# Four of nine FFN down products per chunk as three half products, with one slot more of lag

## The chip, the cores and the metric

The kernel runs on one core of one Trainium2 chip. The time is the device time of one execution in microseconds (us). The core has five engines with a queue of instructions each: TensorE (PE: matmuls; its weight loads stand apart as PEld), VectorE (DVE), ScalarE (ACT), GpSimd (POOL) and SyncE (SP), which here only issues DMAs. An engine takes its instructions strictly in the order in which the program wrote them, and waits on semaphores between them.

## The reference

`x` is 32 x 256 x 128 in float32, that is 8192 tokens of 128 features. What is computed:

```
xn   = layernorm(x)
h,g  = split(xn @ W_hg)                     # 256 + 256
rec  = scan over time: r_t = (1-sigmoid(g_t)) * r_(t-1) + sigmoid(g_t) * (relu(h_t)+0.5)
s    = rec @ W_out
probs = softmax(xn @ Wr)                    # 16 experts, top 2 kept: cw
ffn  = (silu(xn@Sg) * (xn@Su)) @ Sd + sum_e cw_e * (silu(xn@Wg_e) * (xn@Wu_e)) @ Wd_e
out  = x + s * silu(ffn)
```

Two experts of 64 hidden features are handled together as one block of 128, so there are 8 expert blocks and the shared block: nine products `f = 0..8`, each with a gate, a linear and a down product.

## The kernel before

The tokens go in 16 chunks of 512 (`CT`), features on the 128 partitions. The program is written out by hand as one queue per engine. `chunks()` emits chunks 0 and 1, a loop over pairs of chunks, and the last two. Each chunk has 11 slots, `k = 0..10`. In every slot TensorE does `up(k)`: a gate and a linear product, each as three matmuls of float32r halves (`split_product`, lines 604 to 609: hi*hi, lo*hi, hi*lo; x and the weights stand as a rounded high half and a remainder). Slots 0 and 1 are the recurrent part, slots 2 to 10 the nine FFN products, `f = k - 2`. Gates and linears have two PSUM buffers each, so `up(k)` waits for what read the buffers of `up(k-2)`: ScalarE's `silu` (line 319) for the gate, VectorE's `gated` (line 435: `prod = p_lin * silu_g`) for the linear. VectorE's `weighted` (line 445) multiplies `prod` by the expert weight `cw` in SBUF, in place; both of its inputs are in SBUF.

The down product of `f` (line 677) is one float32 matmul of 512 columns (the trace shows it as two records). It accumulates in `p_ffn` and stands `LAG = 3` slots after the product's own slot: at the end of PE slot `f + 5`, so that `f = 6, 7, 8` fall in slots 0, 1, 2 of the next chunk. Its hidden rows come from `weighted`.

Around the chunk boundary, with `ch` the chunk in hand:

- slot 0: TensorE transposes x of the next chunk into `p_front` (L616), which needs `xn`, normalised by VectorE in slots 8 and 9 of the chunk before (L397). ScalarE copies it out (`x_hi`, L297), then does `rec_in(0)` (L302, L304, L307, L309); VectorE does `x_lo` (L404).
- slots 1 and 2: router logits on TensorE (L622), copied by ScalarE (`copy_lgT`, L323), transposed by TensorE (L630). `rec_in(1)` is ahead of that copy in ScalarE's queue.
- after the last down product of the former chunk ScalarE does `ffn_silu` (L340) and VectorE `gate_out` (L508: `sg = p_rec * ffn_gate`). `rec_down(0)` (L687, PE slot 4) overwrites `p_rec` and so waits for `gate_out`. `transpose_out` (L697) and VectorE's `add_out` (L514) follow.
- slot 4 on VectorE: `ln_stats` (L381) of the chunk after the next waits for `x_in` from HBM. The router's steps on the next chunk (L450 to L501) stand between the products. ScalarE's `router_silus` (L328) waits for VectorE's L462, which is behind `ln_stats`, and `silu(5)` is behind `router_silus`.
- slot 10: TensorE transposes the expert weights (L638), ScalarE copies them (L336), and SP writes them to HBM and spreads them over the partitions with four DMAs (L223, 512 KB each). The next `x_in` (L188) is issued behind those on the same SP queue.
- GpSimd only does `rstd_of` (two instructions on 4 columns, L252 and L254) once a chunk.

Of the kernel before, what the change touches and what calls it, by code (L numbers as in the profile page):

```python
# [17 lines left out]
SLOTS = NH + NF  # L18
LAG = 3


class Chunk:
# [17 lines left out]
def recurrent_moe_block(nc, x, W_hg, W_out, Wr, Wg, Wu, Wd, Sg, Su, Sd, out):  # L40
# [13 lines left out]
    with ExitStack() as ctx:  # L54
        def sb(name, shape, dt=F32):
            return ctx.enter_context(nc.sbuf_tensor(name, shape, dt))

        def sem(name):
            return ctx.enter_context(nc.semaphore(name))
# [174 lines left out]
        @block.gpsimd  # L234
        def _(pool):
            nc.gpsimd.memset(minus_half[:, :], -0.5).then_inc(s_const, 1)
            nc.gpsimd.memset(ident[:, :], 0.0).then_inc(s_const0, 1)
            pool.wait_ge(s_const0, 1)
            nc.gpsimd.affine_select(out=ident[:, :], in_=ident[:, :], compare_op=ALU.not_equal, fill=1.0, base=0,
                                    pattern=[[-1, P]], channel_multiplier=1).then_inc(s_const, 1)  # L240
            nc.gpsimd.iota(iota_e[:, :], [[1, E]], base=0, channel_multiplier=0,
                           allow_small_or_imprecise_dtypes=True).then_inc(s_const, 1)
            for col, value in enumerate((-1.0, 1.0, 0.5)):
                nc.gpsimd.memset(consts[:, col:col + 1], value).then_inc(s_const, 1)
            nc.gpsimd.memset(eps[:, :], 1e-5).then_inc(s_const, 1)
# [11 lines left out]
            rstd_of(Chunk(0, 1))  # L257

            def chunk(ch, c):
                if has(c, 2):  # L260
                    rstd_of(ch.at(2))

            chunks(pool, chunk)

        @block.scalar
        def _(act):
# [65 lines left out]
            def copy_cwT(ch, reused):  # L332
# [2 lines left out]
                    act.wait_ge(s_cws, ch.at(-1).n(16, 16))  # L335
                nc.scalar.activation(cwT[:, :], p_out[0:E * TT, 0:P], ACT.Copy).then_inc(s_cwT, 1)  # L336

            def ffn_silu(ch):
                act.wait_ge(s_down, ch.n(NF, NF))
                nc.scalar.activation(ffn_gate[:, :], p_ffn[:, :], ACT.Silu).then_inc(s_gsil, 1)  # L340
# [10 lines left out]
            def chunk(ch, c):  # L351
                late = 1 if c == 0 else 0
                for k in range(SLOTS):
                    if c == 0 and k == 1:
                        router_silus(ch)
                        split_hi(("g", "u"))
                        copy_cwT(ch, False)
                    if k == late and has(c, 1):
                        x_hi(ch.at(1))
                    if k == 2 + late and has(c, 1):  # L360
                        copy_lgT(ch.at(1))
                    if k == 3 and has(c, -1):
                        ffn_silu(ch.at(-1))
                    if k == 5 and has(c, 1):
                        router_silus(ch.at(1))
                    if k < NH:
                        rec_in(ch, k)
                    else:
                        silu(ch, k, c)
                    if k == 10 and has(c, 1):  # L370
                        copy_cwT(ch.at(1), True)

            chunks(act, chunk)
            ffn_silu(Chunk(NCH // 2 - 1, 1))

        @block.vector
        def _(dve):
# [164 lines left out]
            def chunk(ch, c):  # L542
                ahead, ahead2, behind = has(c, 1), has(c, 2), has(c, -1)
                late = 1 if c == 0 else 0
                for k in range(SLOTS):
# [3 lines left out]
                        rec_scan(ch, k - 1)  # L549
                    if c == 0 and k == 1:  # L550
                        split_lo(("u",))
                    if k == 3 and behind:
                        gate_out(ch.at(-1))
                    if k == 5 and behind:
                        add_out(ch.at(-1))
                    if k == 5 and ahead2:
                        ln_stats_landed(ch.at(2))
# [41 lines left out]
        def _(pe):  # L599
# [66 lines left out]
            def down(ch, k, c):  # L666
# [39 lines left out]
            def chunk(ch, c):  # L706
                ahead, behind = has(c, 1), has(c, -1)
                late = 1 if c == 0 else 0
                for k in range(SLOTS):
# [10 lines left out]
                        transpose_logits(ch.at(1))  # L720
                    if k < LAG and behind:
                        down(ch.at(-1), k - LAG + SLOTS, None)
                    if k == 4 and behind:
                        transpose_out(ch.at(-1), True)
                    if k in (4, 5):
                        rec_down(ch, k - 4, c)
# [33 lines left out]
```

## Time and profile before

| | us |
|---|---|
| median of 3 runs | 468.7 (466.78 to 469.61) |
| the profiled execution | 468.29 |
| its span, first to last instruction | 466.5 |
| TensorE busy | 439.5 (94%) |
| VectorE busy | 347.2 (74%) |
| ScalarE busy | 200.0 (43%) |
| GpSimd busy | 25.4 (5%) |

The columns of the timelines shown below are: start in us from the span's start, duration in us, engine, line, operation, output<-inputs, shapes, count, and in brackets the idle time before it and who ended it. Matmul durations include a modelled tail of the pipeline, so the time a matmul takes from its engine is read from start to start.

### The profile page before, as it was taken

The numbers are of one execution on the slowest core, as the hardware profiler recorded it, in microseconds if no ns is written. First come the engines' busy times: TensorE is split into PE (matmuls) and PEld (weight loads), VectorE is DVE, ScalarE is ACT, GpSimd is POOL, SyncE is SP. The second block draws the span as 40 slices with busy tenths as digits, with TensorE's granted clock in tenths as the row PEclk, the third lists the DMA queues.
The fourth block names the chain that finished last, engine by engine and source line by source line (L and its number), as shares of the span: only waits on it lengthen the run. The fifth ranks groups of instructions, "written<-read, shape, count | busy, mean of one in ns | idle before, by whom it ended". The sixth has DMA issues, their size and how long they took to land.

```text
span 466.5 us, 6269 instructions
## 1 busy us (share of the span) xinstructions
PE 439.5 (94%) x1648; PEld 286.4 (61%) x1648; DVE 347.2 (74%) x983; ACT 200.0 (43%) x375; POOL 25.4 (5%) x45
## 2 busy tenths in 40 slices
PE   0787999999899999999999999999999999999995
PEld 0454666656566665666666666666656666666762
DVE  2857678697677968777796877769687776977663
ACT  2722634336163352725335272633527263362621
POOL 1101000010100101010010101001010100100000
PEclk9988999999999999999999999999999999999999
DMA  9091461907528092552809255280925528081640
GB/s 213 22 194 31 102 148 36 196 22 154 98 59 168 25 194 54 125 125 56 171 25 194 53 132 118 58 169 25 193 54 130 120 57 171 26 184 43 140 90 22
DMA packets 50204, 48.98 MB, mean 105 GB/s; under 512 B 6416, under 2 KB 33680, under 8 KB 50192
## 3 DMA queue, kind: packets, MB, share of 16 engines
q1 hardware_dynamic: 44032, 46.67, 46.3%
q10 hardware_dynamic: 6160, 2.17, 2.3%
q8 instruction: 5, 0.08, 0.1%
q14 instruction: 7, 0.06, 0.0%
HBM read 44.11 MB, written 4.72 MB: 105 GB/s over the span
## 4 chain that ended last, share of the span: by engine, by line
PE 56%; DMA 19%; SPq 4%; DVE 2%; issue 2%; ACT 2%; ACTq 0%
PE p_ffn L677 17%; DMA x_in<-in_L_attn_x 16%; PE p_gate L607 6%; PE p_lin L607 6%; PE p_lin L609 5%; PE p_gate L608 5%; PE p_gate L609 5%; PE p_lin L608 5%; SPq L223 4%; DMA cw_scratch<-cwT 3%; PE p_rec L687 3%; ACT silu_g L319 1%; DVE stats L381 1%; PE p_out L697 1%; DVE prod L445 1%
## 5 line engine op out<-in xcount | busy, mean ns | idle before, releaser
L677 PE MATMUL p_ffn<-prod,w_down 128*128 128x512 f32 x288 | 148.7, 599 | 0.0
L319 ACT ACTIVATE silu_g<-p_gate 128x512 f32<-128x512 f32 x144 | 83.8, 592 | 120.2 <-PE p_gate L609 108.3
L607 PE MATMUL p_gate<-xT_hi,w_hi 128*128 128x512 f32 x176 | 124.3, 707 | 8.3 <-ACT silu_g L319 5.6
L435 DVE TENSOR_TENSOR prod<-p_lin,silu_g 128x512 f32<-128x512 f32 x144 | 97.8, 679 | 12.9 <-PE p_lin L609 9.9
L445 DVE TENSOR_TENSOR prod<-prod,cw 128x512 f32<-128x512 f32 x128 | 86.6, 676 | 4.3 <-DMA cw<-cw_scratch 1.8
L607 PE MATMUL p_lin<-xT_hi,w_hi 128*128 128x512 f32 x176 | 71.7, 407 | 0.0
L609 PE MATMUL p_gate<-xT_hi,w_lo 128*128 128x512 f32 x176 | 70.0, 398 | 0.0
L609 PE MATMUL p_lin<-xT_hi,w_lo 128*128 128x512 f32 x176 | 69.9, 397 | 0.0
L608 PE MATMUL p_gate<-xT_lo,w_hi 128*128 128x512 f32 x176 | 69.8, 397 | 0.0
L608 PE MATMUL p_lin<-xT_lo,w_hi 128*128 128x512 f32 x176 | 69.7, 396 | 0.0
L607 PEld LDWEIGHTS p_gate<-xT_hi,w_hi 128*128 128x128 f32 x176 | 33.6, 191 | 51.9 <-issue 28.6
L677 PEld LDWEIGHTS p_ffn<-prod,w_down 128*128 128x128 f32 x288 | 52.2, 189 | 20.7 <-issue 9.1
L608 PEld LDWEIGHTS p_gate<-xT_lo,w_hi 128*128 128x128 f32 x176 | 33.7, 191 | 31.6 <-issue 30.9
L381 DVE BATCH_NORM_STATS2 stats<-x_in 128x6 f32<-128x128 f32 x64 | 14.0, 280 | 45.4 <-DMA x_in<-in_L_attn_x 45.4
L420 DVE SCALAR_TENSOR_TENSOR rec_v<-rec_v,rec_z 128x512 f32<-128x512 f32 x32 | 22.1, 692 | 33.5 <-ACT rec_z L309 33.5
L328 ACT ACTIVATE silu_n<-shifted,consts 128x64 f32<-128x64 f32 x16 | 5.6, 347 | 84.6 <-DVE shifted L462 84.6
L426 DVE TENSOR_TENSOR_SCAN rec_h<-rec_a,rec_v 128x256 f32<-128x256 f32 x64 | 40.8, 678 | 1.1
L607 PEld LDWEIGHTS p_lin<-xT_hi,w_hi 128*128 128x128 f32 x176 | 33.4, 190 | 11.4 <-DVE prod L435 4.2
L609 PEld LDWEIGHTS p_lin<-xT_hi,w_lo 128*128 128x128 f32 x176 | 33.5, 190 | 8.4
L609 PEld LDWEIGHTS p_gate<-xT_hi,w_lo 128*128 128x128 f32 x176 | 33.3, 189 | 7.7
L608 PEld LDWEIGHTS p_lin<-xT_lo,w_hi 128*128 128x128 f32 x176 | 33.5, 190 | 7.3
L687 PE MATMUL p_rec<-rec_h,w_down 128*128 128x512 f32 x64 | 32.7, 592 | 0.0
(60 smaller groups left out, 360.9 us busy)
## 6 DMA issues: line engine op xcount, KB each, us to landing
cw<-cw_scratch SPq DMA_DIRECT2D x64, 512.0 KB, 8.5
x_in<-in_L_attn_x SPq DMA_DIRECT2D x16, 256.0 KB, 10.6
x_out<-in_L_attn_x SPq DMA_DIRECT2D x16, 256.0 KB, 10.6
out_x<-x_out SPq DMA_DIRECT2D x16, 256.0 KB, 2.3
prod<-in_L_ffn_Wg ACTq DMA_DIRECT2D x1, 512.0 KB, 5.9
prod<-in_L_ffn_Wu ACTq DMA_DIRECT2D x1, 512.0 KB, 7.8
w_down<-in_L_ffn_Wd ACTq DMA_DIRECT2D x1, 512.0 KB, 4.5
cw_scratch<-cwT SPq DMA_DIRECT2D x16, 32.0 KB, 1.8
```

Source lines behind the costliest of these rows:

```text
L223: sp.dma_start(cw[e * F:(e + 1) * F, ch.par, b0:b1, :], spread_rows)\
L319: nc.scalar.activation(silu_g[:, par], p_gate[par][:, :], ACT.Silu).then_inc(s_silu, 1)
L381: last = nc.vector.bn_stats(stats[:, t], x_in[:, ch.par, t])
L420: nc.vector.scalar_tensor_tensor(out=rec_v[:, j], in0=rec_v[:, j], scalar=0.5, in1=rec_z[:, j], op0=ALU.add, op1=ALU.mult).then_inc(s_v, 1)
L426: last = nc.vector.tensor_tensor_scan(rec_h[:, j, w], rec_a[:, j, w], rec_v[:, j, w], 0.0, ALU.mult, ALU.add)
L435: nc.vector.tensor_tensor(prod[:, f], p_lin[par][:, :], silu_g[:, par], ALU.mult).then_inc(s_p, 1)
L445: nc.vector.tensor_tensor(prod[:, f], prod[:, f], cw[:, ch.par, f - 1], ALU.mult).then_inc(s_q, 1)
L607: nc.tensor.matmul(acc, w_hi[:, w], hi, start=start, stop=False)
L608: nc.tensor.matmul(acc, w_hi[:, w], lo, start=False, stop=False)
L609: return nc.tensor.matmul(acc, w_lo[:, w], hi, start=False, stop=stop)
L677: nc.tensor.matmul(p_ffn[:, :], w_down[:, at0:at0 + P], prod[:, f], start=f == 0, stop=f == NF - 1)\
L687: last = nc.tensor.matmul(p_rec[:, :], w_down[:, at0:at0 + P], rec_h[:, j], start=j == 0, stop=j == NH - 1)
```

## The change

- `SPLIT = (2, 4, 6, 8)`: the down products of these four `f` are done as three float32r matmuls into the same `p_ffn`: hi weight * hi product, lo weight * hi product, hi weight * lo product.
- The high half of the product (`prod_hi`) is a copy by ScalarE, from SBUF to SBUF; the low half (`prod_lo = prod - prod_hi`) a subtraction by GpSimd with both inputs in SBUF. Both have two buffers. The halves of the weights are made once, at the start.
- The copy for `f` stands in ScalarE's queue at slot `f + 3`, behind that slot's `silu`; for `f = 8` that is slot 0 of the next chunk, between `rec_in(0)` and `rec_in(1)`.
- `LAG = 4`: every down product stands one slot later on TensorE. `ffn_silu` and `gate_out` move from slot 3 to 4, `transpose_out` from 4 to 5, `add_out` from 5 to 6. `rec_down` stays in slots 4 and 5.
- GpSimd's `rstd_of` now stands behind the first of the four subtractions of its chunk.

```diff
-LAG = 3
+LAG = 4
+SPLIT = (2, 4, 6, 8)
...
+            def product_lo(ch, n, c):
+                f = SPLIT[n]
+                pool.wait_ge(s_phi, ch.n(NS, n + 1))
+                if n >= 2:
+                    pool.wait_ge(s_down, ch.n(NF, SPLIT[n - 2] + 1))
+                elif has(c, -1):
+                    pool.wait_ge(s_down, ch.at(-1).n(NF, SPLIT[n + NS - 2] + 1))
+                nc.gpsimd.tensor_tensor(prod_lo[:, n % 2], prod[:, f], prod_hi[:, n % 2].bitcast(F32), ALU.subtract)\
+                  .then_inc(s_plo, 1)
+
             def chunk(ch, c):
-                if has(c, 2):
-                    rstd_of(ch.at(2))
+                for n in range(NS):
+                    if n == 1 and has(c, 2):
+                        rstd_of(ch.at(2))
+                    product_lo(ch, n, c)
...
+            def product_hi(ch, n, known):
+                f = SPLIT[n]
+                act.wait_ge(s_q, ch.n(NB, f))
...
+                nc.scalar.activation(prod_hi[:, n % 2], prod[:, f], ACT.Copy).then_inc(s_phi, 1)
...
-                    if k == 3 and has(c, -1):
+                    if k == 4 and has(c, -1):
                         ffn_silu(ch.at(-1))
...
+                    if k == 0 and has(c, -1):
+                        product_hi(ch.at(-1), NS - 1, True)
+                    for n, f in enumerate(SPLIT):
+                        if k == f + NH + 1:
+                            product_hi(ch, n, has(c, -1))
...
-                    if k == 3 and behind:
+                    if k == 4 and behind:
                         gate_out(ch.at(-1))
-                    if k == 5 and behind:
+                    if k == 6 and behind:
                         add_out(ch.at(-1))
...
+                elif f in SPLIT:
+                    n = SPLIT.index(f)
...
+                    pe.wait_ge(s_plo, ch.n(NS, n + 1))
+                    w = slice(n * P, (n + 1) * P)
+                    nc.tensor.matmul(p_ffn[:, :], down_hi[:, w], prod_hi[:, n % 2], start=False, stop=False)
+                    nc.tensor.matmul(p_ffn[:, :], down_lo[:, w], prod_hi[:, n % 2], start=False, stop=False)
+                    nc.tensor.matmul(p_ffn[:, :], down_hi[:, w], prod_lo[:, n % 2], start=False, stop=f == NF - 1)\
+                      .then_inc(s_down, 1)
+                    return
...
-                    if k == 4 and behind:
+                    if k == 5 and behind:
                         transpose_out(ch.at(-1), True)
```

**TensorE, slots 3 and 4 of a chunk in the loop.** Six matmuls with `p_gate` and `p_lin` are one `up`; in brackets stands what an instruction waits for. Before, from the end of `up(2)`'s down product on:

```order
L607 MATMUL p_gate<-xT_hi,w_hi 128x512 [waits tanh_done]
L608 MATMUL p_gate<-xT_lo,w_hi 128x512
L609 MATMUL p_gate<-xT_hi,w_lo 128x512
L607 MATMUL p_lin<-xT_hi,w_hi 128x512 [waits relu_done]
...
L607 MATMUL p_gate<-xT_hi,w_hi 128x512 [waits silu_done]
...
L607 MATMUL p_lin<-xT_hi,w_hi 128x512 [waits gated_done]
...
L695 REGISTER_ALU [waits sg_done]
L697 MATMUL p_out<-ident,sg 128x128 [waits cwT_copied]
L697 MATMUL p_out<-ident,sg 128x128 x3
L687 MATMUL p_rec<-rec_h,w_down 128x512 [waits scan_done,sg_done]
```

and now, for the same two slots:

```order
L658 MATMUL p_gate<-xT_hi,w_hi 128x512 [waits tanh_done]
...
L658 MATMUL p_lin<-xT_hi,w_hi 128x512 [waits relu_done]
...
L731 MATMUL p_ffn<-prod_hi,down_hi 128x512 [waits product_lo_ready]
L732 MATMUL p_ffn<-prod_hi,down_lo 128x512
L733 MATMUL p_ffn<-prod_lo,down_hi 128x512
L658 MATMUL p_gate<-xT_hi,w_hi 128x512 [waits silu_done]
...
L658 MATMUL p_lin<-xT_hi,w_hi 128x512 [waits gated_done]
...
L749 MATMUL p_rec<-rec_h,w_down 128x512 [waits scan_done,sg_done]
```

The last down product of the former chunk (`f = 8`) now stands behind `up(3)`. Before, two `up`s stood between it and the first instruction that waits for `sg`; now it is one.

**VectorE, slots 3 and 4 of the same chunk.** Before:

```order
L435 TENSOR_TENSOR prod<-p_lin,silu_g 128x512 [waits linear_in_psum]
L506 REGISTER_ALU
L508 TENSOR_TENSOR sg<-p_rec,ffn_gate 128x512 [waits rec_out_done,ffn_gate_done]
L434 REGISTER_ALU [waits silu_done]
L435 TENSOR_TENSOR prod<-p_lin,silu_g 128x512 [waits linear_in_psum]
L450 TENSOR_REDUCE lg<-p_front 128x64 [waits router_logits]
L453 ISA
L445 TENSOR_TENSOR prod<-prod,cw 128x512 [waits gated_done,cw_first_half1,router_step]
L457 MAX top<-lg 128x8 x4
```

and now:

```order
L486 TENSOR_TENSOR prod<-p_lin,silu_g 128x512 [waits linear_in_psum]
L501 TENSOR_REDUCE lg<-p_front 128x64 [waits router_logits]
L504 ISA
L496 TENSOR_TENSOR prod<-prod,cw 128x512 [waits gated_done,cw_first_half1,router_step]
L508 MAX top<-lg 128x8 x4
L557 REGISTER_ALU
L559 TENSOR_TENSOR sg<-p_rec,ffn_gate 128x512 [waits rec_out_done,ffn_gate_done]
```

`sg` was made ahead of `gated(3)`; now it comes behind `gated(3)`, the router's sum, `weighted(3)` and the router's maximum.

**ScalarE, slots 0 and 1.** Now (before, the rows with `prod_hi` and the REGISTER_ALU ahead of it were not there):

```order
L336 ACTIVATE rec_z<-rec_z,consts 128x512
L373 REGISTER_ALU
L378 ACTIVATE prod_hi<-prod 128x512 [waits down_done,weighted_done]
L328 REGISTER_ALU
L329 ACTIVATE rec_z<-p_gate 128x512 [waits gate_in_psum]
L331 ACTIVATE rec_v<-p_lin 128x512 [waits linear_in_psum]
L333 REGISTER_ALU
L334 ACTIVATE rec_a<-rec_z,consts 128x512 [waits tanh_done]
L336 ACTIVATE rec_z<-rec_z,consts 128x512
L350 ACTIVATE lgT<-p_front 32x512 [waits router_logits_T]
```

The copy for `f = 8` stands ahead of `rec_in(1)` and of the copy of the logits, which TensorE's L630 (now L681) waits for.

## Rows read from the trace of the kernel before

**Rows 1.** The page, busy time and share of the span.

```profile
PE 439.5 (94%) x1648; PEld 286.4 (61%) x1648; DVE 347.2 (74%) x983; ACT 200.0 (43%) x375; POOL 25.4 (5%) x45
```

**Rows 2.** Timeline of TensorE, a down product and the gate product behind it.

```profile
210.47 1.02 PE L677 MATMUL p_ffn<-prod,w_down 128*128 128x512 f32 x2
...
211.55 0.39 PE L608 MATMUL p_gate<-xT_lo,w_hi 128*128 128x512 f32 x1
211.78 0.40 PE L609 MATMUL p_gate<-xT_hi,w_lo 128*128 128x512 f32 x1
```

**Rows 3.** The page, chain of work that ended last, shares of the span.

```profile
PE 56%; DMA 19%; SPq 4%; DVE 2%; issue 2%; ACT 2%; ACTq 0%
```

**Rows 4.** The waits, in total, times and longest.

```profile
DVE stats L381 <- DMA x_in<-in_L_attn_x: 45.4, 15, 4.5
```

**Rows 5.** Timeline of TensorE, the transposition of the expert weights, once a chunk.

```profile
214.96 0.27 PE L638 MATMUL p_out<-ident,cw_tok 128*128 128x128 f32 x1
242.14 0.27 PE L638 MATMUL p_out<-ident,cw_tok 128*128 128x128 f32 x1
...
405.31 0.27 PE L638 MATMUL p_out<-ident,cw_tok 128*128 128x128 f32 x1
432.05 0.27 PE L638 MATMUL p_out<-ident,cw_tok 128*128 128x128 f32 x1
```

**Rows 6.** Timeline of TensorE in the chunk from 214.96 on.

```profile
222.83 0.43 PE L630 MATMUL p_front<-ident,lgT 32*128 32x32 f32 x4
...
226.93 0.60 PE L697 MATMUL p_out<-ident,sg 128*128 128x128 f32 x4
...
232.72 1.02 PE L677 MATMUL p_ffn<-prod,w_down 128*128 128x512 f32 x2
233.72 0.50 PE L607 MATMUL p_gate<-xT_hi,w_hi 128*128 128x512 f32 x1
```

**Rows 7.** Timeline of ScalarE in the same chunk.

```profile
221.32 0.71 ACT L309 ACTIVATE rec_z<-rec_z,consts 128x512 f32<-128x512 f32 x1
221.94 0.57 ACT L323 ACTIVATE lgT<-p_front 32x512 f32<-32x512 f32 x1
...
233.09 1.06 ACT L319 ACTIVATE silu_g<-p_gate 128x512 f32<-128x512 f32 x2
```

**Rows 8.** Timeline of VectorE in the same chunk.

```profile
224.98 0.69 DVE L508 TENSOR_TENSOR sg<-p_rec,ffn_gate 128x512 f32<-128x512 f32 x1 [0.33 <-ACT ffn_gate L340]
225.76 0.69 DVE L435 TENSOR_TENSOR prod<-p_lin,silu_g 128x512 f32<-128x512 f32 x1
...
227.61 0.67 DVE L435 TENSOR_TENSOR prod<-p_lin,silu_g 128x512 f32<-128x512 f32 x1
230.97 0.87 DVE L381 BATCH_NORM_STATS2 stats<-x_in 128x6 f32<-128x128 f32 x4 [2.68 <-DMA x_in<-in_L_attn_x]
...
233.07 0.67 DVE L514 TENSOR_TENSOR x_out<-p_out,x_out 128x512 f32<-128x512 f32 x1
233.85 0.69 DVE L435 TENSOR_TENSOR prod<-p_lin,silu_g 128x512 f32<-128x512 f32 x1
...
235.02 0.66 DVE L445 TENSOR_TENSOR prod<-prod,cw 128x512 f32<-128x512 f32 x1
...
235.73 0.68 DVE L435 TENSOR_TENSOR prod<-p_lin,silu_g 128x512 f32<-128x512 f32 x1
...
241.51 0.59 DVE L397 TENSOR_SCALAR xn<-x_in,meanvar,rstd 128x128 f32<-128x128 f32 x2
```

**Rows 9.** Timeline of GpSimd, start of the program and the same chunk.

```profile
1.22 0.29 POOL L239 TENSOR_SCALAR_AFFINE_SELECT ident<-ident 128x128 f32<-128x128 f32 x1 [0.24 <-POOL ident L237]
...
5.48 0.20 POOL L252 TENSOR_TENSOR var_eps<-meanvar,eps 128x4 f32<-128x4 f32 x1 [3.64 <-DVE meanvar L389]
...
235.18 0.55 POOL L252 TENSOR_TENSOR var_eps<-meanvar,eps 128x4 f32<-128x4 f32 x1 [25.54 <-DVE meanvar L389]
```

**Rows 10.** Timeline of TensorE, the last four down products of the program.

```profile
457.33 3.59 PE L677 MATMUL p_ffn<-prod,w_down 128*128 128x512 f32 x8
```

More of the change, by code:

```diff
@@ L99, in recurrent_moe_block @@
         rec_h = sb("rec_h", [P, NH, CT])
+        NS = len(SPLIT)
+        down_hi = sb("down_hi", [P, NS * P], F32R)
+        down_lo = sb("down_lo", [P, NS * P], F32R)
+        prod_hi = sb("prod_hi", [P, 2, CT], F32R)
+        prod_lo = sb("prod_lo", [P, 2, CT], F32R)
         silu_g = sb("silu_g", [P, 2, CT])
@@ L154, in recurrent_moe_block @@
         s_down = sem("down_done")
+        s_dwhi, s_dwlo = sem("down_weights_hi"), sem("down_weights_lo")
+        s_phi, s_plo = sem("product_hi_ready"), sem("product_lo_ready")
         s_rec, s_gsil, s_sg, s_ot, s_add = (sem("rec_out_done"), sem("ffn_gate_done"), sem("sg_done"),
@@ L257, in _ @@
             rstd_of(Chunk(0, 1))
+            for n, f in enumerate(SPLIT):
+                w = slice(down_at["d"] + (f - 1) * P, down_at["d"] + f * P)
+                pool.wait_ge(s_dwhi, n + 1)
+                nc.gpsimd.tensor_tensor(down_lo[:, n * P:(n + 1) * P], w_down[:, w],
+                                        down_hi[:, n * P:(n + 1) * P].bitcast(F32), ALU.subtract).then_inc(s_dwlo, 1)
+            def product_lo(ch, n, c):
[7 more added lines that the diff above has]
+                  .then_inc(s_plo, 1)
             def chunk(ch, c):
-                if has(c, 2):
-                    rstd_of(ch.at(2))
+                for n in range(NS):
+                    if n == 1 and has(c, 2):
+                        rstd_of(ch.at(2))
+                    product_lo(ch, n, c)
             chunks(pool, chunk)
@@ L336, in copy_cwT, with down_weights_hi @@
                 nc.scalar.activation(cwT[:, :], p_out[0:E * TT, 0:P], ACT.Copy).then_inc(s_cwT, 1)
+            def down_weights_hi():
+                act.wait_ge(s_w["d"], 16)
+                for n, f in enumerate(SPLIT):
+                    w = slice(down_at["d"] + (f - 1) * P, down_at["d"] + f * P)
+                    nc.scalar.activation(down_hi[:, n * P:(n + 1) * P], w_down[:, w], ACT.Copy).then_inc(s_dwhi, 1)
+            def product_hi(ch, n, known):
+                f = SPLIT[n]
+                act.wait_ge(s_q, ch.n(NB, f))
+                if n >= 2:
+                    act.wait_ge(s_down, ch.n(NF, SPLIT[n - 2] + 1))
+                elif known:
+                    act.wait_ge(s_down, ch.at(-1).n(NF, SPLIT[n + NS - 2] + 1))
+                nc.scalar.activation(prod_hi[:, n % 2], prod[:, f], ACT.Copy).then_inc(s_phi, 1)
             def ffn_silu(ch):
@@ L357, in chunk @@
                         copy_cwT(ch, False)
+                    if c == 0 and k == 2:
+                        down_weights_hi()
                     if k == late and has(c, 1):
@@ L371, in chunk @@
                         copy_cwT(ch.at(1), True)
+                    if k == 0 and has(c, -1):
+                        product_hi(ch.at(-1), NS - 1, True)
+                    for n, f in enumerate(SPLIT):
+                        if k == f + NH + 1:
+                            product_hi(ch, n, has(c, -1))
             chunks(act, chunk)
-            ffn_silu(Chunk(NCH // 2 - 1, 1))
+            last = Chunk(NCH // 2 - 1, 1)
+            product_hi(last, NS - 1, True)
+            ffn_silu(last)
         @block.vector
@@ L673, in down @@
                     pe.wait_ge(s_p, ch.n(NF, 1))
+                elif f in SPLIT:
+                    n = SPLIT.index(f)
+                    if c == 0:
+                        pe.wait_ge(s_dwlo, n + 1)
+                    pe.wait_ge(s_plo, ch.n(NS, n + 1))
[5 more added lines that the diff above has]
+                    return
                 else:
```

## The prediction

> **What bounds the kernel now.** I read the page's busy shares first: TensorE 94%, nobody else over 74% [rows 1]. So TensorE looks like the bound, and a change that takes work from it looks good. The chain of waits says less: 56% TensorE, 19% DMA [rows 3]. The list of waits names it: VectorE waits for `x_in` 15 times, 45.4 us in all [rows 4]. The timeline shows what this does. A chunk, measured between two transpositions of the expert weights, takes 242.14 - 214.96 = 27.18 us; the one chunk that loads no `x_in` takes 432.05 - 405.31 = 26.74 [rows 5]. Expert weights, their spread and `x_in` form a line: `x_in` is there 230.97 - 214.96 = 16.01 us after the transposition [rows 5, 8]; then come `ln_stats`, `weighted(4)`, the router's shift, ScalarE's router silus and `silu(5)`, of which TensorE's gate of slot 7 waits until 233.72, while its down product at 232.72 was over 0.86 later, at 233.58 [rows 6]. So a chunk is a stretch A of 18.76 us (to the gate of slot 7), with 18.62 of TensorE's own work and a floor at 18.76 set by the DMAs, and a stretch B of 8.42 us. TensorE's own work in B is four `up`s of 6 x 0.233 = 1.40 and three down products of 0.86, 8.18; the rest, 0.24, is waiting behind the late `silu` and `gated`.
>
> **What it saves.** Start to start, half matmuls are 0.23 apart (211.78 - 211.55). The gate behind the down product began at 211.55 - 0.23 = 211.32, so the float32 product takes 211.32 - 210.47 = 0.85 to 0.86 [rows 2]. Three halves take 0.69 or 0.70. That saves 0.16 each, 64 x 0.16 = 10.2 us in all, if TensorE never waits. Per chunk: three of the four (`f = 4, 6, 8`) fall in A, 0.48, which takes TensorE's work there to 18.14, below the floor; one (`f = 2`) in B.
>
> **ScalarE's copies.** A 512 column instruction from SBUF follows its neighbour by 221.94 - 221.32 = 0.62 [rows 7]; I take 0.61. Three of the four per chunk stand where ScalarE idles. That of `f = 8` does not: it pushes `rec_in(1)` and the copy of the logits. The copy ended at 221.94 + 0.57 = 222.51, just ahead of TensorE's L630 at 222.83 [rows 6, 7]. Now it ends 0.61 later, less the 0.16 by which all of slot 0 is early: 222.96. TensorE has saved two halves' worth by then and wants it at 222.51; it starts at 223.0. **Wait: 0.5.** It could be as little as 0.3 if the copy overlaps its neighbours.
>
> **`sg`.** Slot 3's `up` ended at 226.93 - 1.40 = 225.53; now at 225.53 - 0.32 + 0.5 = 225.7. `gated(3)` started 0.23 after that (225.76), and VectorE was through with slot 3 at 227.61, 1.85 later [rows 8]. Only then comes `gate_out`, 0.69: 225.7 + 0.23 + 1.85 + 0.69 = 228.5. TensorE has `f = 8` (0.69) and `up(4)` (1.40) meanwhile and wants `sg` for `rec_down(0)` at 227.8. **Wait: 0.7**, where before `sg` was ready at 225.67, over 1 us early. It depends on no unknown price. A becomes 18.62 - 0.48 + 0.5 + 0.7 = 19.35, over the floor of 18.76 by 0.6. `x_in` itself stays where it was.
>
> **B without further trouble.** The 0.24 of waiting goes, since TensorE is late itself; one half product: 8.18 - 0.16 = 8.02. A chunk: 19.35 + 8.02 = **27.4**, against 27.18: the whole saving is gone, with 0.2 more.
>
> **GpSimd beside VectorE.** This is the large unknown. The trace has no GpSimd instruction of 512 columns. Its select on 128 columns takes 0.29, some 1.5 ns a column beyond 0.1; its two-input add on 4 columns 0.20 [rows 9]. That makes 0.20 + 512 x 1.5 ns = 1.0 us for a subtraction; bounds are 0.6 (near VectorE's 0.69 for this shape) and 1.7 (each input read in turn). TensorE has over 2 us of slack for each. But the same add takes 0.55 at 235.18: VectorE's `weighted`, two inputs in SBUF, ran from 235.02 to 235.68, and the add ended at 235.73 [rows 8, 9]. GpSimd sat out VectorE's whole instruction; the two exclude each other. The trace cannot show the reverse, as a read of 4 columns holds nothing up. Bounds of what a subtraction costs VectorE: nothing, or its whole duration. I take the exclusion to hold both ways, since it lasted to the end of the holder's instruction.
>
> The subtraction becomes ready about 0.7 after its `weighted`, while VectorE is in the next `gated` (one input in SBUF), and the next `weighted` or mask stands behind it: some 0.85 of 1.0 us each. Three fall in the stretch from `x_in` to the second half of `xn`, the third only partly: C = 2.0 us.
>
> Does VectorE have room for that? From 230.97 to the end of `xn` at 242.10 it hardly pauses [rows 8]. Before, `add_out` (233.07) filled the time until `silu(5)` was over at 233.09 + 0.57 = 233.66, and `gated(5)` started at 233.85 [rows 7, 8]. In the new order `gated(5)` waits for the same `silu(5)`, and `add_out` is paid behind it: some 0.5 later, so `xn` is ready 16.01 + 11.13 + 0.5 + C = 27.6 + C after the transposition. TensorE needs it for the transposition of x, 0.8 after the end of the chunk's period P. If it waits s there, P = 27.4 + s and s = 27.6 + C - P - 0.8, so P = 27.1 + C/2 once C is over 0.6. With C = 2.0: **P = 28.1**.
>
> The Trainium skill, page SBUF — State Buffer, section Who interferes with whom, says that VectorE with two SBUF inputs contends with a GpSimd instruction that reads SBUF, and that whoever issues second fully blocks. This trace agrees in one direction (0.20 against 0.55 us) and shows nothing of the other; by the row alone, with VectorE never blocked, the chunk would stay at 27.4, by the rule it is the 28.1.
>
> The same skill, page GPSIMD Engine Reference, section Performance versus the Vector engine, gives 4497 ns for a two-input add of 2048 columns; a quarter is an estimate of 1.1 us, and no run here shows it. By it the sum would be about 1 us longer.
>
> **The rest.** Thirteen chunks have the steady form (C = 0: 13 x 0.2 = 2.9). Chunk 14 has no `x_in` and loses 1.2 to the two waits against 0.64 saved: +0.6. The last has no router: -0.5; in its tail, four down products took 8 records at 0.43 = 3.43 [rows 10]; now the last `weighted`, 1.7 after slot 10, is followed by copy 0.6, subtraction 1.0 and three halves 0.7, 4.1: +0.7. Weight halves at the start: four small copies and subtractions while TensorE waits anyway, 0. Two late `x_in`s of the thirteen are partly covered now: -0.8. Sum without contention: 2.9 + 0.6 - 0.5 + 0.7 - 0.8 = +2.9. With C = 2.0: 13 x 0.7 = 9.1 more, +12. The profiled execution took 468.29, 0.4 below the median: 480.3 by it, **481** by the median.
>
> **The rivals.** *(1) VectorE isn't blocked*: GpSimd alone gives way. For it: only that direction is in the trace. Then +2.9, **472**. *(2) It pays*: the two waits vanish, because VectorE reaches `gate_out` in time and the logits' copy slips in. Then A sits on its floor of 18.76 and B costs 8.02: 26.78, 13 x -0.4 = -5.2, the ends about -1: **462**. It is decided by `gate_out` ending before 227.8; against it stand three queued VectorE instructions. If even the floor gave way the full saving would lead to 458. *(3) Subtraction at its upper bound of 1.7*: C = 3.5, P = 28.9, **491**.
>
> **Chances.** Forecast (C from 1 to 3, 474 to 488) 0.52; rival 1 0.30; rival 2 0.12; rival 3 0.06. A measurement of this kernel tells about 1%, 4.7 us. The range of 466 to 490 leaves out rival 2 and half of the upper tail. Faster by over 1% (below 464): 0.12. Within 1%: rival 1 but for a rest, 0.28. Slower: 0.60.
>
> **What would show it.** Right: TensorE waits at the transposed logits (L681) some 0.5 and at `rec_down(0)` (L749) some 0.7 a chunk, the latter for `sg`; `weighted` (L496) with durations well over 0.69, or gaps before it; chunk period 28.1. VectorE's wait for `x_in` shrinks. Wrong: `weighted` still at 0.68 throughout (rival 1), no wait at L749 (rival 2), subtractions of more than 1.5 us (rival 3). The prediction also fails if blocking is traded against VectorE's idle time in slots 0 to 4 more than I assume.

## The result: 7% slower, and the profile after

The changed kernel takes 501.49 us (median of 4 runs, 500.56 to 504.06), the kernel before 469.15 (4 runs, 466.78 to 471.53): a ratio of 1.0701, 95% interval 1.0664 to 1.0738. The direction was forecast, the size was not: 32 us were lost where 12 were expected, and the range ended at 490. The profiled execution took 501.97 us with a span of 500.2, against 468.29 and 466.5.

I read the page first: busy times, then the shares of the chain of waits.

```profile
PE 434.4 (87%) x1712; PEld 296.2 (59%) x1712; DVE 410.4 (82%) x983; ACT 231.8 (46%) x443; POOL 111.5 (22%) x113
...
DMA 30%; issue 17%; DVE 17%; PE 9%; ACT 6%; SPq 6%; ACTq 1%; DVEq 0%; POOLq 0%
...
L281 POOL TENSOR_TENSOR prod_lo<-prod,prod_hi 128x512 fp32r<-128x512 f32 x64 | 82.6, 1290 | 352.4 <-ACT prod_hi L378 326.2
...
L496 DVE TENSOR_TENSOR prod<-prod,cw 128x512 f32<-128x512 f32 x128 | 106.5, 832 | 3.9 <-DMA cw<-cw_scratch 1.3
```

VectorE has the same 983 instructions as in [rows 1] and is busy for 410.4 us instead of 347.2. That is 63.2 us more for 64 subtractions on another engine, 1.0 us each. A subtraction takes 1.29 us. TensorE, 56% of the chain in [rows 3], now has 9%: it no longer sets the time, although its queue is busy for 87% of the span.

The waits (in total, times, longest):

```profile
ACT prod_hi L378 <- DVE prod L496: 70.5, 29, 3.7
...
PE p_front L667 <- DVE xn L448: 31.4, 15, 8.1
...
DVE stats L432 <- DMA x_in<-in_L_attn_x: 25.3, 15, 4.0
...
PE p_rec L749 <- DVE sg L559: 9.6, 15, 0.8
...
PE p_front L681 <- ACT lgT L350: 5.3, 14, 0.4
```

The two waits of TensorE that the forecast named are there (0.4 at L681, 0.6 at L749 a chunk), and VectorE's for `x_in` has shrunk from the 45.4 of [rows 4]. On top, TensorE waits for `xn`, and ScalarE's copy waits for `weighted`. The period, by the transposition of the expert weights (timeline of TensorE; compare [rows 5]):

```profile
198.03 0.27 PE L689 MATMUL p_out<-ident,cw_tok 128*128 128x128 f32 x1
...
227.66 0.27 PE L689 MATMUL p_out<-ident,cw_tok 128*128 128x128 f32 x1
...
257.18 0.27 PE L689 MATMUL p_out<-ident,cw_tok 128*128 128x128 f32 x1
```

A chunk takes 29.5 us, not 27.2. This chunk on VectorE (the lines that were stretched, with the `x_in` at either end):

```profile
215.24 0.87 DVE L432 BATCH_NORM_STATS2 stats<-x_in 128x6 f32<-128x128 f32 x4 [1.07 <-DMA x_in<-in_L_attn_x]
...
218.67 1.32 DVE L537 TENSOR_TENSOR mask<-iota_e,top_at 128x64 f32<-128x64 f32 x1
...
224.17 1.84 DVE L496 TENSOR_TENSOR prod<-prod,cw 128x512 f32<-128x512 f32 x1
...
227.37 0.68 DVE L496 TENSOR_TENSOR prod<-prod,cw 128x512 f32<-128x512 f32 x1
228.57 1.69 DVE L448 TENSOR_SCALAR xn<-x_in,meanvar,rstd 128x128 f32<-128x128 f32 x2
...
235.06 2.34 DVE L477 TENSOR_TENSOR_SCAN rec_h<-rec_a,rec_v 128x256 f32<-128x256 f32 x2
238.02 1.27 DVE L477 TENSOR_TENSOR_SCAN rec_h<-rec_a,rec_v 128x256 f32<-128x256 f32 x2
...
244.77 0.87 DVE L432 BATCH_NORM_STATS2 stats<-x_in 128x6 f32<-128x128 f32 x4 [1.12 <-DMA x_in<-in_L_attn_x]
```

and GpSimd in the same stretch:

```profile
218.65 1.27 POOL L281 TENSOR_TENSOR prod_lo<-prod,prod_hi 128x512 fp32r<-128x512 f32 x1 [12.01 <-ACT prod_hi L378]
...
224.16 1.30 POOL L281 TENSOR_TENSOR prod_lo<-prod,prod_hi 128x512 fp32r<-128x512 f32 x1 [2.02 <-PE p_ffn L733]
228.89 1.30 POOL L281 TENSOR_TENSOR prod_lo<-prod,prod_hi 128x512 fp32r<-128x512 f32 x1 [3.43 <-ACT prod_hi L378]
234.98 1.29 POOL L281 TENSOR_TENSOR prod_lo<-prod,prod_hi 128x512 fp32r<-128x512 f32 x1 [4.79 <-ACT prod_hi L378]
```

Each subtraction has one VectorE record beside it that is too long by most of the subtraction's duration: the mask by 1.1 (0.22 otherwise), `weighted` by 1.16 (0.68 at 227.37), `xn` by 1.1 (0.59 in [rows 8]), the scans by 1.07 (1.27 at 238.02). The line behind a stretched record never starts before the subtraction has ended: right at its end behind the mask (219.92) and `xn` (230.19), 0.5 us later behind `weighted`, 1.1 behind the scans. GpSimd blocks VectorE as VectorE blocked GpSimd in [rows 9].

The Trainium skill, page SBUF — State Buffer, section Who interferes with whom, says that the two share a port pair as an exclusive lock, held for the whole instruction by whoever issues first. This trace now agrees in both directions, with 0.68 against 1.84 us for the same shape on VectorE.

**The loop that holds the chunk** goes through the one place where ScalarE's copies hurt (timeline of ScalarE):

```profile
228.09 0.63 ACT L378 ACTIVATE prod_hi<-prod 128x512 fp32r<-128x512 f32 x1 [2.64 <-DVE prod L496]
228.62 0.58 ACT L346 ACTIVATE silu_g<-p_gate 128x512 f32<-128x512 f32 x1
229.10 0.26 ACT L363 ACTIVATE cwT<-p_out 64x128 f32<-64x128 f32 x1
```

`x_in` lands at 215.24. VectorE, blocked twice on the way, reaches the end of the `weighted` of 227.37 at 228.05. ScalarE has stood 2.64 us at `prod_hi` for `f = 6` for it. Behind that in its queue are `silu(10)` and `copy_cwT`, though TensorE's transposition was done shortly after 227.66. `copy_cwT` releases the expert weights' spread and, on the same SP queue, the next `x_in`, which lands 15.67 us after 229.10. So 215.24 to 229.10 is 13.86, and 13.86 + 15.67 = 29.53, the period. TensorE is not in this loop. Measured from the transposition, `x_in` lands 244.77 - 227.66 = 17.11 us later, in the kernel before 16.01.

### The profile page after: what moved, and what is told of

It is laid out like the page before. It is cut to its first block, busy times and chain, and to the rows that moved or that the text cites. A ratio compares the mean times of both kernels' runs of the same rounds, so it can differ in the third digit from the quotient of the medians.

```text
span 500.2 us, 6755 instructions
## 1 busy us (share of the span) xinstructions
PE 434.4 (87%) x1712; PEld 296.2 (59%) x1712; DVE 410.4 (82%) x983; ACT 231.8 (46%) x443; POOL 111.5 (22%) x113
## 4 chain that ended last, share of the span: by engine, by line
DMA 30%; issue 17%; DVE 17%; PE 9%; ACT 6%; SPq 6%; ACTq 1%; DVEq 0%; POOLq 0%
DMA x_in<-in_L_attn_x 24%; SPq L232 5%; DMA cw_scratch<-cwT 4%; DVE prod L496 4%; ACT silu_g L346 4%; DVE prod L486 3%; DVE xn L448 2%; DVE x_out L565 2%; DVE stats L432 2%; DMA cw<-cw_scratch 1%; PE p_ffn L739 1%; PE p_rec L749 1%; PE p_gate L660 1%; PE p_gate L658 1%; PE p_gate L659 1%
## 5 line engine op out<-in xcount | busy, mean ns | idle before, releaser
L281 POOL TENSOR_TENSOR prod_lo<-prod,prod_hi 128x512 fp32r<-128x512 f32 x64 | 82.6, 1290 | 352.4 <-ACT prod_hi L378 326.2
L658 PE MATMUL p_gate<-xT_hi,w_hi 128*128 128x512 f32 x176 | 115.0, 653 | 6.0 <-ACT silu_g L346 3.2
L496 DVE TENSOR_TENSOR prod<-prod,cw 128x512 f32<-128x512 f32 x128 | 106.5, 832 | 3.9 <-DMA cw<-cw_scratch 1.3
L739 PE MATMUL p_ffn<-prod,w_down 128*128 128x512 f32 x160 | 83.6, 604 | 0.0
L378 ACT ACTIVATE prod_hi<-prod 128x512 fp32r<-128x512 f32 x64 | 40.0, 625 | 72.1 <-DVE prod L496 70.5
L477 DVE TENSOR_TENSOR_SCAN rec_h<-rec_a,rec_v 128x256 f32<-128x256 f32 x64 | 56.9, 929 | 1.1
L749 PE MATMUL p_rec<-rec_h,w_down 128*128 128x512 f32 x64 | 34.3, 617 | 9.6 <-DVE sg L559 9.6
L667 PE MATMUL p_front<-ident,xn 128*128 128x128 f32 x64 | 10.9, 294 | 31.8 <-DVE xn L448 31.4
```

The lines of the kernel that those rows point to most:

```text
L281: nc.gpsimd.tensor_tensor(prod_lo[:, n % 2], prod[:, f], prod_hi[:, n % 2].bitcast(F32), ALU.subtract)\
L378: nc.scalar.activation(prod_hi[:, n % 2], prod[:, f], ACT.Copy).then_inc(s_phi, 1)
L477: last = nc.vector.tensor_tensor_scan(rec_h[:, j, w], rec_a[:, j, w], rec_v[:, j, w], 0.0, ALU.mult, ALU.add)
L496: nc.vector.tensor_tensor(prod[:, f], prod[:, f], cw[:, ch.par, f - 1], ALU.mult).then_inc(s_q, 1)
L658: nc.tensor.matmul(acc, w_hi[:, w], hi, start=start, stop=False)
L739: nc.tensor.matmul(p_ffn[:, :], w_down[:, at0:at0 + P], prod[:, f], start=f == 0, stop=f == NF - 1)\
```

## The experiments

Two theories were open at first: the *loop* just read, and *TensorE's own* waits with contention only on top. Each run is set against the kernel before, run on the same chip.

**lo_4cols: contention taken away.** GpSimd subtracts 4 columns.

```
-                nc.gpsimd.tensor_tensor(prod_lo[:, n % 2], prod[:, f], prod_hi[:, n % 2].bitcast(F32), ALU.subtract)\
+                nc.gpsimd.tensor_tensor(prod_lo[:, n % 2, 0:4], prod[:, f, 0:4], prod_hi[:, n % 2, 0:4].bitcast(F32), ALU.subtract)\
```

> The changed kernel, but GpSimd subtracts only the first 4 of the 512 columns of each product (the low half of the other columns stays zero, so the output lacks those corrections); every wait, copy and matmul is kept. It takes the 1.1 us blocks of VectorE away (the subtraction is about 0.2 us long) and nothing else. Theory (GpSimd holding VectorE up carries nearly all of the loss; the two new waits of TensorE cost 0.2 us a chunk): 470 to 475 us, as the forecast's sum without contention, 472. Rival (the lag, ScalarE's copies and the longer queue carry a good part): 480 us or more, with TensorE still waiting for xn at the transposition of x.

475.40 us, ratio 1.0146 (1.0107 to 1.0185); period 27.5. VectorE busy is 348.1, back at that of before. The edit also makes the subtraction itself shorter, but TensorE waits for `prod_lo` only once in the changed kernel, 0.5 us at the end. So 26 of the 32 us are contention. What is left fits the forecast's chunk without contention, 27.4, and TensorE's waits are those it named (waits):

```profile
PE p_rec L754 <- DVE sg L564: 9.7, 15, 0.8
...
PE p_front L686 <- ACT lgT L355: 5.3, 14, 0.4
```

It also gives the length of the loop (timelines of VectorE and ScalarE, in this order):

```profile
233.34 0.88 DVE L437 BATCH_NORM_STATS2 stats<-x_in 128x6 f32<-128x128 f32 x4 [2.09 <-DMA x_in<-in_L_attn_x]
...
244.07 0.63 ACT L383 ACTIVATE prod_hi<-prod 128x512 fp32r<-128x512 f32 x1 [1.55 <-DVE prod L501]
```

From `x_in` to this copy 244.07 - 233.34 = 10.73, in the changed kernel 228.09 - 215.24 = 12.85. The two blocks inside cost 2.12 of the 2.26 by which their records are longer, and 29.5 - 2.1 = 27.4: by this sum the loop without them is about as long as TensorE's chunk, so that every further block in it counts in full.

**lag4_only: the later slot alone**, the kernel before with `LAG = 4` and the four slots moved.

```
-LAG = 3
+LAG = 4
```

> The kernel before with LAG = 4 and the four stages moved with it; no halves, nothing new on ScalarE or GpSimd. Theory: rec_down(0) waits for sg, since VectorE reaches gate_out 2.8 us after up(3) and TensorE gets there in 2.3; 0.4 to 0.6 us a chunk, of which 0.14 was waiting before: 471 to 476 us. Rival (the expert weights and x_in set the pace and hide it): 468 to 470.

475.81 us, 1.0151 (1.0113 to 1.0189); period 27.5. The wait for `sg` is there without any copy or subtraction:

```profile
PE p_rec L687 <- DVE sg L508: 6.5, 14, 0.6
```

The later slot loses 7 us by itself. lo_4cols, which has it too, saves 0.64 a chunk on TensorE, but waits 0.4 for the logits and 0.65 instead of 0.46 for `sg`, and so takes the same time.

**split_lag3: the split without the later slot.** `ffn_silu`, `gate_out`, `transpose_out` and `add_out` are back in their slots of before.

```
-LAG = 4
+LAG = 3
```

> The changed kernel with LAG = 3 and ffn_silu, gate_out, transpose_out and add_out in their slots of before; halves, copies and subtractions kept. Theory (the loop through VectorE, ScalarE and the DMAs sets the period, so TensorE's waits for sg, 0.7 us a chunk, cost nothing now): 498 to 503 us, as the changed kernel, with no wait at rec_down(0). Rival (each of TensorE's waits adds to the sum): 489 to 492.

492.86 us, 1.0517 (1.0470 to 1.0564): 9 less than the change. The theory missed (498 to 503), and the time is within 1 us of what the rival named (489 to 492: each of TensorE's waits adds), so it does not decide between them. The chain of waits does (page); it is still that of the loop:

```profile
DMA 28%; DVE 21%; issue 17%; PE 12%; ACT 6%; SPq 6%; ACTq 0%; DVEq 0%; POOLq 0%; POOL 0%
```

I had missed where `add_out` goes (timeline of VectorE):

```profile
211.23 0.87 DVE L432 BATCH_NORM_STATS2 stats<-x_in 128x6 f32<-128x128 f32 x4 [1.81 <-DMA x_in<-in_L_attn_x]
...
213.34 0.67 DVE L565 TENSOR_TENSOR x_out<-p_out,x_out 128x512 f32<-128x512 f32 x1
...
240.24 0.87 DVE L432 BATCH_NORM_STATS2 stats<-x_in 128x6 f32<-128x128 f32 x4 [1.96 <-DMA x_in<-in_L_attn_x]
```

`add_out` is back where VectorE waits anyway (in the change it stands at 221.06, inside the loop). `copy_cwT` is at 224.49, 13.26 behind `x_in` instead of 13.86. The DMAs then take 240.24 - 224.49 = 15.75, so this chunk is 29.0 long instead of 29.5: 13 x 0.5 = 6.5 of the 9.

**cwT_first: the loop's ScalarE part cut.** `prod_hi` of `f = 6` goes behind `silu(10)` and `copy_cwT`.

```
-                        if k == f + NH + 1:
+                        if k == f + NH + (2 if f == 6 else 1):
```

> The changed kernel, but ScalarE's copy of the product f = 6 stands one slot later, behind the copy of the transposed expert weights (cwT) instead of ahead of it. Theory (a loop without TensorE sets the period: x_in lands, VectorE works to weighted(8), ScalarE's copy waits for it with silu(10) and the copy of cwT queued behind it, so SP issues the next x_in late): the cwT copy starts 0.4 us after TensorE's transposition instead of 1.4, x_in comes 1 us earlier, and the chunk falls from 29.5 to 28.5 to 28.9 us: 488 to 494 us. Rival (the copy of cwT is late but not on the path, as VectorE's own blocks set the pace through xn): 500 to 502, unchanged.

489.36 us, 1.0429 (1.0381 to 1.0477); period about 28.5. One copy moved, 12 us back. Timelines of TensorE, ScalarE, VectorE and GpSimd, in this order:

```profile
223.60 0.27 PE L689 MATMUL p_out<-ident,cw_tok 128*128 128x128 f32 x1
...
223.99 0.27 ACT L363 ACTIVATE cwT<-p_out 64x128 f32<-64x128 f32 x1 [0.36 <-PE p_out L689]
...
224.51 0.59 DVE L448 TENSOR_SCALAR xn<-x_in,meanvar,rstd 128x128 f32<-128x128 f32 x2
...
226.34 1.07 DVE L496 TENSOR_TENSOR prod<-prod,cw 128x512 f32<-128x512 f32 x1
...
224.95 1.90 POOL L281 TENSOR_TENSOR prod_lo<-prod,prod_hi 128x512 fp32r<-128x512 f32 x1 [3.56 <-ACT prod_hi L378]
```

`copy_cwT` now starts 0.39 after the transposition (in the change 1.44). And the later subtraction meets `xn` second: `xn` keeps its 0.59, it is the subtraction that takes 1.90, and it holds only the `weighted` of 226.34, by 0.4. So the edit shortens the loop's ScalarE part by 1.05 and also takes a block away from `xn`, and the 12 us are not the first alone. That the loop holds the changed kernel rests on its waits, one at each link, and on x_early_after below, where the DMA link alone is cut. What is left here, 20 us, is not split up; TensorE waits for `xn` (17.2 us in 14 times, 8.1 of them once), the logits and `sg`.

**dve_lo: the subtractions on VectorE itself**, one slot behind the copy.

```
-                nc.gpsimd.tensor_tensor(prod_lo[:, n % 2], ...)
+                nc.vector.tensor_tensor(prod_lo[:, n % 2], ...)
```

> The changed kernel, but VectorE does the subtraction itself, behind weighted of slot f + 4 (f = 8: slot 1 of the next chunk); GpSimd is as in the kernel before. VectorE pays 4 x 0.61 = 2.4 us a chunk instead of four blocks of 1.1. Two of the four stand ahead of the second half of xn. Theory (VectorE's time between x_in and xn, and the cwT copy behind the copy of product 6, set the loop): chunk about 27.9 to 28.3, 478 to 485 us, well below the 501 of the changed kernel, with no long weighted. Rival (VectorE's extra work is as bad as GpSimd's blocks): 495 or more.

486.94 us, 1.0375 (1.0352 to 1.0398), a little over what I expected. The instruction takes 681 ns there (group of instructions):

```profile
L562 DVE TENSOR_TENSOR prod_lo<-prod,prod_hi 128x512 fp32r<-128x512 f32 x64 | 43.6, 681 | 0.1
```

VectorE is busy for 383.7 us, 27 less than with the work "taken off" it. GpSimd's help costs VectorE more than doing the work itself, and the kernel 15 us more.

**pool_reads and pool_reads_late: contention alone.** The kernel before, with four GpSimd subtractions of 512 columns a chunk on idle tiles. In the first they are released by `weighted`; in the second three of them by the `gated` behind it, which is about when the change's subtractions start.

```
+                    nc.gpsimd.tensor_tensor(spare[:, :], w_down[:, 0:CT], w_down[:, CT:2 * CT], ALU.subtract)
```

```
-                    pool.wait_ge(s_q, ch.n(NB, 2 * n + 2))
+                    if n < 3:
+                        pool.wait_ge(s_p, ch.n(NF, 2 * n + 4))
+                    else:
+                        pool.wait_ge(s_q, ch.n(NB, NB))
```

> The kernel before, plus four GpSimd subtractions of 512 columns per chunk on spare data (weights in SBUF, result unused), each released by weighted(2), (4), (6), (8). No copy on ScalarE, no change of lag, TensorE's work as before. It measures the disputed cost by itself. Theory (GpSimd's reads hold up VectorE's instructions whatever data they read): weighted, the mask, xn and the scan get durations 0.6 to 1.1 us above their own, and the chunk grows from 27.2 to 27.6 to 28.3 us: 474 to 484 us. Rival (the loss of the changed kernel comes from ScalarE's queue alone): 468 to 471 us.

470.82 us, 1.0020 (0.9996 to 1.0043): my expectation missed, nothing is lost. Timeline of VectorE, then of GpSimd:

```profile
264.38 1.15 DVE L456 TENSOR_TENSOR prod<-prod,cw 128x512 f32<-128x512 f32 x1
...
268.10 1.26 DVE L408 TENSOR_SCALAR xn<-x_in,meanvar,rstd 128x128 f32<-128x128 f32 x2
...
263.71 1.28 POOL L272 TENSOR_TENSOR spare<-w_down 128x512 f32<-128x512 f32 x1 [0.76 <-DVE prod L456]
267.74 1.28 POOL L272 TENSOR_TENSOR spare<-w_down 128x512 f32<-128x512 f32 x1 [2.75 <-DVE prod L456]
```

The subtraction at 263.71 starts right behind a `weighted`, and VectorE is in `gated` (one input from PSUM), untouched. Only the rest of it meets the next `weighted`: 1.15 instead of 0.65. `xn` pays 0.67. That is 1.17 in all, and the kernel takes it up: TensorE waits for `xn` only at the start of the program (waits).

```profile
PE p_front L627 <- DVE xn L408: 8.2, 1, 8.2
```

By the forecast's numbers the room before TensorE waits is 27.18 + 0.8 - (16.01 + 11.13) = 0.84. So I asked whether the start decides:

> The kernel before plus the same four GpSimd subtractions on spare data, but those of products 2, 4 and 6 are released 0.6 us later: by gated of the next slot instead of by weighted itself, which is about where the changed kernel starts them behind ScalarE's copy. Released by weighted they cost nothing (470.8 us). Theory (a subtraction of 1.29 us holds VectorE for what is left of it when VectorE's next instruction with two SBUF inputs, or xn, comes; begun behind weighted half of it passes beside gated, begun behind gated nearly all is waited for): instructions of VectorE stretched by 1.1 to 1.2 us three times between x_in and xn, chunk 27.9 to 28.4: 479 to 487 us. Rival (the placing makes no difference, only ScalarE's queue does): 469 to 473.

480.83 us, 1.0241 (1.0205 to 1.0277); period 28.1. Timeline of VectorE, then of GpSimd:

```profile
266.83 1.53 DVE L459 TENSOR_TENSOR prod<-prod,cw 128x512 f32<-128x512 f32 x1
...
271.55 1.31 DVE L509 TENSOR_TENSOR mask<-mask,expv 128x64 f32<-128x64 f32 x1
...
266.53 1.29 POOL L275 TENSOR_TENSOR spare<-w_down 128x512 f32<-128x512 f32 x1 [15.12 <-DVE prod L449]
```

The same four instructions, three of them started later against VectorE's sequence, cost 10 us: VectorE is busy for 390.7 us, against 362.0 in pool_reads. So the blocks alone, with no copy and no later slot, make the kernel slower.

**x_early_before and x_early_after: the DMA link cut.** SP issues each `x_in` a chunk earlier, behind the store and ahead of the spread of the expert weights, in the kernel before and in the changed one; the loop over chunk pairs ends one pair earlier.

```
-                if has(c, 2):
+                if c == 0:
                     load_x(ch.at(2))
...
                     store(ch.at(-1))
+                if has(c, 3):
+                    load_x(ch.at(3))
```

> The kernel before with x_in loaded one chunk earlier: SP issues it ahead of the spread of the expert weights instead of behind it (the loop is one pair of chunks shorter and that pair written out, for the index). Theory (in the kernel before each chunk pays 0.4 us for x_in being late behind the spread): every chunk takes the 26.7 us of the one that loads no x_in, VectorE's wait for x_in is gone: 459 to 464 us. Rival (something else, the spread itself or VectorE's own work, stands right behind): 466 to 469.

460.36 us, 0.9797 (0.9781 to 0.9813); period 26.75, that of the one chunk without `x_in` in [rows 5]. TensorE has 90% of the chain.

> The changed kernel with x_in loaded one chunk earlier in the same way; GpSimd's subtractions and all else kept. It cuts the loop x_in, VectorE, ScalarE, spread, x_in at one place. Theory (the blocks of VectorE only cost because they stand in that loop; VectorE's idle wait for x_in then takes them in): the chunk falls from 29.5 to 27.2 to 27.7 us, TensorE's own work plus the waits for the logits and sg: 470 to 478 us. Rival (the blocks hit TensorE directly, by xn and gated): 488 or more.

483.40 us, 1.0291 (1.0274 to 1.0309); period about 28.4. The time lies between theory and rival: 18 us are back, with VectorE blocked as before (busy for 409.0 us), but a second loop takes over. Timeline of TensorE, then of VectorE:

```profile
220.95 0.65 PE L671 MATMUL p_front<-ident,xn 128*128 128x128 f32 x4 [0.79 <-DVE xn L452]
249.26 0.65 PE L671 MATMUL p_front<-ident,xn 128*128 128x128 f32 x4 [0.77 <-DVE xn L452]
...
231.07 0.69 DVE L490 TENSOR_TENSOR prod<-p_lin,silu_g 128x512 f32<-128x512 f32 x1 [0.65 <-PE p_lin L664]
...
247.41 1.71 DVE L452 TENSOR_SCALAR xn<-x_in,meanvar,rstd 128x128 f32<-128x128 f32 x2
```

From the transposition of x TensorE takes 10.1 us to the linear product of the VectorE line at 231.07; from there VectorE, blocked three times, takes 18.05 to the end of `xn` at 249.12. With the 0.14 to TensorE that is 28.3. This is not the forecast's path either: that one also ended at `xn`, but it ran through the DMAs and `x_in` and took two chunks (P = 27.1 + C/2).

**x_early_4cols and all_off: is the saving real?** The first is lo_4cols with the early `x_in`. The second also puts the copy for `f = 8` two slots later and `rec_down` one slot later, which takes away TensorE's two waits.

```
-                    if k == 0 and has(c, -1):
+                    if k == 2 and has(c, -1):
                         product_hi(ch.at(-1), NS - 1, True)
...
-                    if k in (4, 5):
-                        rec_down(ch, k - 4, c)
+                    if k in (5, 6):
+                        rec_down(ch, k - 5, c)
```

> The changed kernel with x_in loaded one chunk earlier and GpSimd's subtraction on 4 of the 512 columns (the low half of the other columns stays zero): neither the loop through the DMAs nor the blocks, but both of TensorE's new waits. Theory (what is left are the two waits, 0.4 for the copied logits and 0.75 for sg, against 0.64 saved): chunk 27.2 to 27.4, 468 to 472 us, 8 to 11 above the kernel before with early x_in (460). Rival (the waits are partly the effect of blocks and late x_in): 460 or less.

471.42 us, 1.0032 (1.0015 to 1.0049); period 27.4, against 27.5 in lo_4cols: in both TensorE with its two waits holds the chunk. Of the 4 us between the two, 2 fall in a single chunk near the start (29.20 and 27.33).

> As x_early_4cols, and the two waits taken away too: ScalarE's copy of product 8 stands in slot 2 behind the copy of the logits, and rec_down in slots 5 and 6 instead of 4 and 5. Theory (the saving of 0.16 us per product is real and is seen once nothing else is in the way): chunk 26.75 - 0.64 = 26.1 us, 449 to 453 us. Rival (three half products between other matmuls don't save TensorE 0.16 us): 458 or more.

451.96 us, 0.9609 (0.9581 to 0.9637), 8.4 less than x_early_before:

```profile
233.44 0.27 PE L698 MATMUL p_out<-ident,cw_tok 128*128 128x128 f32 x1
259.54 0.27 PE L698 MATMUL p_out<-ident,cw_tok 128*128 128x128 f32 x1
```

26.1 against 26.75 a chunk: the 4 x 0.16 = 0.64 of the half products, whole, once nothing else is in TensorE's way.

**all_off_real: the same with all 512 columns subtracted.**

> As all_off, but GpSimd subtracts all 512 columns: the whole change, with early x_in, the copy of product 8 behind the logits, and rec_down one slot later. The blocks of VectorE are back, and nothing else. Theory (a second loop holds it: from the transposition of x TensorE needs 9.6 us to lin(3), VectorE from there 18 us to xn, of which 3.3 are blocks): chunk 27.6 to 28.0, 472 to 479 us. Rival (with x_in early VectorE's slack takes the blocks in): under 462.

475.01 us, 1.0112 (1.0081 to 1.0143); period about 27.9. Of TensorE's waits in the loop only that for `xn` is left:

```profile
PE p_front L671 <- DVE xn L452: 27.8, 15, 8.1
```

All the moves that help cannot pay for the subtractions on GpSimd: 23 us between 4 columns and 512. The version that beats both kernels is x_early_before, the kernel before with its `x_in` issued early.

## Why the prediction was right and wrong

**Right.**

- The two waits of TensorE: 0.37 and 0.55 in the chunk shown, against 0.5 and 0.7 forecast. The chunk without contention is 27.5 (lo_4cols), summed as 27.4, and lo_4cols is at 475 where the sum gave 472. lag4_only shows that the later slot brings the `sg` wait.
- The saving of 0.16 a product is real (all_off).
- The exclusion holds both ways; rival 1 (VectorE isn't blocked, 472) falls with the 1.84 us of `weighted`. Rival 2 (the two waits vanish, 462) falls with TensorE's waits. Rival 3 wanted a subtraction over 1.5 us: at 1.29 it isn't that, though its 491 was nearest.

**The step that failed: "`x_in` itself stays where it was".** It rested on "Three of the four per chunk stand where ScalarE idles". That of `f = 6` does stand in idle time, but it *waits* there for `weighted`, with `silu(10)` and `copy_cwT` queued behind it. `copy_cwT` comes 1.44 after the transposition starts instead of 0.39, and the time of `x_in` hangs on VectorE: it lands 17.11 after the transposition, not 16.01. I took P = 27.1 + C/2, a loop in which TensorE passes on half of what VectorE loses. In the one that holds, each block between `x_in` and `prod_hi(6)` counts whole. With my own price of 0.85 for each of the two blocks there, it gives 27.4 + 1.7 = 29.1 where I had 28.1: 13 x 1.0 = 13 us. x_early_after cuts this link, with all blocks kept, and gets 18 us back; cwT_first takes the copy out of the way and gets 12.

**The mis-sized term: the price of a block.** I took 0.85 of a subtraction of 1.0 us; measured are 1.29 and 1.1. The two blocks cost 2.1, not 1.7: 13 x 0.4 = 5 us. C as I defined it, all three up to `xn`, is 1.10 + 1.16 + 1.10 = 3.4, not 2.0; with that, my own formula would give 27.1 + 1.7 = 28.8, 0.7 short of the 29.5 measured: the right price alone would not have mended it. VectorE's path was otherwise as I had it: from `x_in` to the end of `xn` it takes 230.26 - 215.24 = 15.02, and 11.13 + 0.5 + 3.4 is 15.0. The Trainium skill's page GPSIMD Engine Reference, section Performance versus the Vector engine, from which 1.1 us was estimated, is nearer than my 1.0 and still under the 1.29.

**The ends.** Chunk 14, without `x_in`, I had at +0.6; it takes 464.19 - 434.91 = 29.28 against 26.74 [rows 5], +2.5; in it TensorE waits 1.69 for `xn`, which I had not counted there. Behind the last transposition of the expert weights the span has 500.2 - 464.19 = 36.0, before 466.5 - 432.05 = 34.5: +1.5 where I had +0.2 for router and tail. In the tail TensorE waits 0.47 for the last subtraction. (The tail's sum of 4.1 should have been 4.0.) Together the ends make 3 us. With 13 and 5 it is 21 of the 21.7 between the 480.3 forecast for a profiled execution and 501.97.

**A worry that came true the other way round.** That "blocking is traded against VectorE's idle time" holds for pool_reads, where VectorE is only 14.8 us busier and nothing is lost, and not for the change: its subtractions come after ScalarE's copy, just when VectorE turns to its next instruction of the sensitive kind.

**Open.** dve_lo's 28.4 isn't split up; TensorE waits there for `prod_lo` as well (8.7 us in 14 times). A subtraction split into shorter ones was not tried.

## What to carry to other kernels

Work that GpSimd takes over from SBUF isn't off VectorE: price it at up to its full duration there (here 1.1 of 1.29 us), and read from the timeline which instruction it will meet and who starts first. When an instruction that waits is put into an in-order queue, list what is behind it, and follow that through the DMAs to the next round: a loop that bypasses the busiest engine can be the next bound while that engine still shows 87%. Where two loops are about equally long, shortening one gives little: the early `x_in` brings 9 us to the kernel before and 4 to lo_4cols, where TensorE's waits hold the chunk. First move what costs nothing, here a DMA issue.

## What the hardware showed that I had not expected

- Which VectorE instructions GpSimd's 1.3 us subtraction blocks: not only those with two SBUF inputs (0.68 to 1.84, scans 1.27 to 2.34) but also `xn`, a tensor_scalar with one tensor input from SBUF to SBUF (0.59 to 1.69). The Trainium skill's page SBUF — State Buffer, section Who interferes with whom, names tensor_scalar as able to take the second port pair; this trace agrees in that it is held (0.59 to 1.69), and doesn't show the port. `gated`, with one input from PSUM, stays at 0.65 to 0.69 throughout.
- A mask of 64 columns, 0.22 us of work, is held 1.1 us as well (1.32): here the price hangs on the holder, not on the one that is held.
- The price depends on where in VectorE's sequence the subtraction starts: 470.8 against 480.8 us for the same four a chunk. In the chunks shown the first starts 1.8 us ahead of the mask and the second 0.1 behind the start of a `gated` (pool_reads); in pool_reads_late they start 0.3 and 0.8 behind the same two.
- It works in either direction within one kernel: `xn` second is 1.69, `xn` first is 0.59 and the subtraction 1.90 (cwT_first).
- GpSimd's two-input fp32 subtraction of 512 columns takes 1.29 us, VectorE's 0.68.
